# GpSimd takes over two small operations of each layer norm in a gated cross-attention kernel

## The reference

```python
x = x + tanh(g_xattn[0]) * L0_xattn(ctx, ctx, layernorm(x), ...)   # layer norm A; softmax over heads
x = x + tanh(g_ffn[0])   * L0_ffn(layernorm(x), ...)               # layer norm B; silu gate, hidden 768
x = x + tanh(g_xattn[1]) * L1_xattn(layernorm(x), ctx, ...)        # layer norm C; softmax over keys
x = x + tanh(g_ffn[1])   * L1_ffn(layernorm(x), ...)               # layer norm D; one linear map
```

```python
def _layernorm(x, axis=-1, eps=1e-05):
    m = jnp.mean(x, axis=axis, keepdims=True)
    v = jnp.var(x, axis=axis, keepdims=True)
    return (x - m) / jnp.sqrt(v + eps)
```

## Time and profile before

| | |
|---|---|
| runs before | 2554.6, 2552.17, 2556.8 us; median 2554.6 us |
| profiled execution | 2554.42 us, its span 2552.6 us |
| TensorE busy | 2463.6 us, 97% |
| VectorE busy | 2311.4 us, 91% |
| ScalarE busy | 1616.7 us, 63% |
| GpSimd busy | 1476.5 us, 58% |
| neg_mean, four norms | 64 each; A 457 ns, D 217 ns, B and C 169 ns on the mean |
| var_eps, four norms | 64 each; 156 to 161 ns |
| granted TensorE clock over the span | 0.996 |

### The profile page before, as it was taken

One profiled execution on the slowest core, in us unless ns is written; L12 is line 12 of the kernel. 1 busy time (PEld: TensorE's weight loads), 2 busy tenths in 40 slices (PEclk: granted clock), 3 DMA queues, 4 the chain that ended last, 5 costly groups with the idle time before them and its releaser, 6 DMA issues.

```text
span 2552.6 us, 70067 instructions
## 1 busy us (share of the span) xinstructions
PE 2463.6 (97%) x27972; PEld 2151.3 (84%) x27972; DVE 2311.4 (91%) x4254; ACT 1616.7 (63%) x3210; POOL 1476.5 (58%) x1806
## 2 busy tenths in 40 slices
PE   6999999999999999999999999999999999999997
PEld 5888888888888888888888888888888888888886
DVE  7889999999999999999999999999999999999974
ACT  4466666666666666666666666666666666666653
POOL 3555565565565565665665665665665665655642
PEclk9999999999999999999999999999999999999999
DMA  3000010010000010010110110110110100110100
GB/s 101 20 28 25 25 33 22 28 33 21 29 31 23 29 31 23 29 31 19 33 31 19 33 31 19 33 31 19 33 31 19 33 31 19 33 31 19 30 18 14
DMA packets 74322, 73.20 MB, mean 29 GB/s; under 512 B 6555, under 2 KB 73393, under 8 KB 74290
## 3 DMA queue, kind: packets, MB, share of 16 engines
q1 hardware_dynamic: 74290, 72.75, 9.2%
HBM read 54.90 MB, written 16.78 MB: 28 GB/s over the span
## 4 chain that ended last, share of the span: by engine, by line
PE 48%; DVE 46%; issue 3%; ACT 1%; POOL 0%; DMA 0%; SPq 0%; POOLq 0%; DVEq 0%; ACTq 0%
PE work L1849 11%; PE work L1850 9%; PE work L1851 9%; DVE m L1284 6%; DVE e L1302 6%; DVE m L1293 5%; PE scores L1952 5%; PE work L1985 5%; DVE x L1321 4%; DVE y_q L1312 3%; PE scores L1942 3%; DVE scores L1290 3%; PE work L1888 3%; PE work L1866 2%; DVE work L1298 2%
## 5 line engine op out<-in xcount | busy, mean ns | idle before, releaser
L731 ACT ACTIVATE e<-scores 120x1024 f32<-120x1024 f32 x512 | 497.4, 1023 | 133.2 <-PE scores L1952 97.0
L1849 PE MATMUL work<-xt_hi_B,w_hi 128*128 128x256 f32 x1536 | 452.4, 295 | 1.9 <-DVE xt_lo_B L1264 0.9
L1851 PE MATMUL work<-xt_hi_B,w_lo 128*128 128x256 f32 x1536 | 432.9, 282 | 0.0
L1850 PE MATMUL work<-xt_lo_B,w_hi 128*128 128x256 f32 x1536 | 432.8, 282 | 0.0
L388 POOL TENSOR_TENSOR h_lo<-h_f,h_hi 128x256 fp32r<-128x256 f32 x384 | 291.4, 772 | 219.7 <-ACT h_hi L681 219.7
L394 POOL TENSOR_TENSOR zt<-e 120x512 f32<-120x512 f32 x256 | 325.8, 1284 | 80.1 <-ACT e L731 80.1
L1849 PEld LDWEIGHTS work<-xt_hi_B,w_hi 128*128 128x128 f32 x1536 | 289.2, 188 | 58.4 <-issue 21.3
L1284 DVE TENSOR_REDUCE m<-scores 120x128 fp32r<-120x2048 f32 x128 | 291.7, 2279 | 3.1 <-PE scores L1942 3.1
L1302 DVE TENSOR_TENSOR e<-e,work 120x2048 f32<-120x2048 f32 x128 | 292.1, 2282 | 2.2
L681 ACT ACTIVATE h_hi<-h_f 128x256 fp32r<-128x256 f32 x384 | 157.1, 432 | 215.2 <-DVE h_f L1278 210.6
L1850 PEld LDWEIGHTS work<-xt_lo_B,w_hi 128*128 128x128 f32 x1536 | 289.5, 188 | 2.8
(11 more groups left out here) (213 smaller groups left out, 7299.1 us busy)
## 6 DMA issues: line engine op xcount, KB each, us to landing
x_res<-xp SPq DMA_DIRECT2D x64, 256.0 KB, 2.8
x_ln<-xp SPq DMA_DIRECT2D x64, 256.0 KB, 2.9
y<-y_out SPq DMA_DIRECT2D x64, 256.0 KB, 2.2
ctx_f_A<-cp SPq DMA_DIRECT2D x64, 128.0 KB, 2.1
ctx_f_C<-cp SPq DMA_DIRECT2D x64, 128.0 KB, 2.0
qm<-mT SPq DMA_DIRECT2D x256, 4.0 KB
e<-wi SPq DMA_DIRECT2D x3, 768.0 KB, 6.9
w_ctx<-wc SPq DMA_DIRECT2D x1, 656.0 KB
```

Source lines behind the costliest of these rows:

```text
L731: return act.activation(e[0:SC, c, 2 * h:2 * h + 2, :, :].rearrange("p a b n -> p (a b n)"), scores[0:SC, 2 * h:2 * h + 2, :].rearrange("p ...
L1849: pe.matmul(out, a_hi, b_hi_, start=first, stop=False, skip_group_check=parts)
L1850: pe.matmul(out, a_hi, b_lo_, start=False, stop=False, skip_group_check=parts)
L1851: last = pe.matmul(out, a_lo, b_hi_, start=False, stop=end, skip_group_check=parts)
```

## The change

In `moments` VectorE no longer writes neg_mean and var_eps and no longer waits for bn_aggr; what follows the norm on other engines now follows the second bn_aggr. In `root` GpSimd first adds a constant tile of epsilon to the two variances, subtracts the two means from a constant tile of zeros, waits for the addition, and then takes the power and the product as before. Two memsets fill the new tiles. The order of the work on each engine stays as it is.

```diff
--- before.py
+++ after.py
@@ -33,7 +33,7 @@
 KC = D // P
 NT = S // P
 HC = HID // P
-INIT_POOL = 9
+INIT_POOL = 11
 FIRST = 2
 STAGES_BEHIND = 0
 CONSTS = 7
@@ -106,6 +106,8 @@
         x3_biased = sb("x3_biased", [P, NT, D])
         val_bias = sb("val_bias", [P, D])
         minus_half = sb("minus_half", [P, NT])
+        eps_tile = sb("eps_tile", [P, NT])
+        zero_tile = sb("zero_tile", [P, NT])
 
         x_ln = sb("x_ln", [P, NT, D])
         x_res = sb("x_res", [P, NT, D])
@@ -365,6 +367,8 @@
         @block.gpsimd
         def _(pool):
             pool.memset(minus_half[:, :], -0.5).then_inc(s["init_pool"], 1)
+            pool.memset(eps_tile[:, :], EPS).then_inc(s["init_pool"], 1)
+            pool.memset(zero_tile[:, :], 0.0).then_inc(s["init_pool"], 1)
             pool.memset(v0_pad[:, :, :], 0.0).then_inc(s["init_pool"], 1)
             pool.memset(v1_one[:, :], 1.0).then_inc(s["init_pool"], 1)
             pool.memset(ones_k[:, :].bitcast(F32), 1.0).then_inc(s["bias_zero"], 1)
@@ -379,9 +383,12 @@
             pool.wait_ge(s["init_pool"], INIT_POOL)
 
             def root(st, t):
+                pool.tensor_tensor(var_eps[st][:, :], mv[st][:, :, 1], eps_tile[:, :], ALU.add).then_inc(s[f"ln_root_{st}"], 1)
+                pool.tensor_tensor(neg_mean[st][:, :], zero_tile[:, :], mv[st][:, :, 0], ALU.subtract)
+                pool.wait_ge(s[f"ln_root_{st}"], within(0, 2, t))
                 pool.tensor_tensor(rstd[st][:, :], var_eps[st][:, :], minus_half[:, :], ALU.pow)\
                     .then_inc(s[f"ln_root_{st}"], 1)
-                pool.wait_ge(s[f"ln_root_{st}"], within(0, 1, t))
+                pool.wait_ge(s[f"ln_root_{st}"], within(1, 2, t))
                 return pool.tensor_tensor(shift[st][:, :], neg_mean[st][:, :], rstd[st][:, :], ALU.mult)
 
             def hidden_lo(m):
@@ -1251,14 +1258,11 @@
                 for i in range(NT):
                     last = dve.bn_stats(stats[st][:, i, :], x[:, i, :])
                 last.then_inc(s[f"ln_mom_{st}"], 1)
-                dve.wait_ge(s[f"ln_mom_{st}"], within(0, 2, t))
+                dve.wait_ge(s[f"ln_mom_{st}"], within(0, 1, t))
                 dve.tensor_copy(ln_count[:, :], stats[st][:, 0, 0:1])
                 for i in range(NT):
                     last = dve.bn_aggr(mv[st][:, i, :], stats[st][:, i, :])
-                last.then_inc(s[f"ln_mom_{st}"], 1)
-                dve.wait_ge(s[f"ln_mom_{st}"], within(1, 2, t))
-                dve.tensor_scalar(neg_mean[st][:, :], mv[st][:, :, 0], -1.0, None, ALU.mult)
-                return dve.tensor_scalar(var_eps[st][:, :], mv[st][:, :, 1], EPS, None, ALU.add)
+                return last
 
             def low(out, src, hi):
                 return dve.tensor_tensor(out, src, hi.bitcast(F32), ALU.subtract)
```

## The result

The changed kernel takes 2511.6 us (median of 4 runs, 2510.54 to 2513.09) against 2554.62 us before (4 runs, 2552.17 to 2556.8): a ratio of 0.9832, 95% interval 0.9815 to 0.9849. It is 43.0 us faster. The forecast was faster, 2526 us and a range of 2518 to 2545: the sign is right, the gain is half as large again as the forecast one and lies outside the range.

A forecast was written before the change was run, and what follows sets the result against it. It took each 38.48 us pass as bound by VectorE, then TensorE, in turn, with the B chain deciding together with f1. Saving 0.49 us over 59 passes, 28.9 us off 2554.4, gave 2526 us, range 2518 to 2545.

The forecast's parts named there:

- The ceiling: TensorE's wait for xt_lo_D before product f1: VectorE savings could gain at most about 0.52 us a pass.
- 0.57 (D and C): VectorE before moments B: savings behind bn_aggr of D (0.31) and C (0.26) start x_res 0.57 us earlier.
- I take 0.35: GpSimd's root: 0.35 us from the add's start to the power's start, add slot 0.15 plus a complete subtract 0.20.
- the TensorE stretch keeps its length: TensorE's part of a pass, after transposes B and gate_up: unchanged in length, so 0.49 us is saved a pass.
- p: Time in GpSimd's root from add to power; the gain a pass is 0.57 + 0.27 - p.
- rival 1: The forecast itself: 0.38 to 0.56 us gained a pass, 2521 to 2532 us, chance 0.6.
- I count nothing: The 20 of 256 layer norms outside the loop: together under some 5 us, put at nothing.
- Rival 2: Added GpSimd work is dearer and part of the gain goes back through shift_B: 2532 to 2549 us, chance 0.16.
- rival 3: Slower: add and subtract each cost what the power costs, B chain 0.54 us later a pass, 2586 us, chance 0.04.
- Rival 4: Saved VectorE time meets another wait (x_res for wo0, or attended products), pass about 38.48 us: 2550 to 2559, chance 0.06.
- Rival 5: More than forecast: shorter first f1 product, p at 0.27, a few us outside the loop; 2514 to 2521 us, chance 0.14.
- signs named for cases 2 and 3: Add or subtract above 0.3 us, or ScalarE's shift_B wait grows and TensorE waits for xn_B or xt_lo_B.

The follow-up runs named there:

- e1: Changed kernel with only norms C and D moved to GpSimd, A and B as before the change: a pass of 37.797 us, 2509.51 us in one run.
- e2: Changed kernel with only norm A moved to GpSimd, the others as before the change: a pass of 38.442 us, 2549.70 us in one run.
- e3: Changed kernel with only norm B moved to GpSimd, the others as before the change: a pass of 38.463 us, 2549.16 us in one run.
- e8: Changed kernel with A, C and D moved and B wholly as before the change: a pass of 37.814 us, 2511.01 us, ratio 0.9831.
- e5: Changed kernel with two more GpSimd subtractions in each of roots A, C and D: a pass of 37.833 us, 2513.56 us in one run.
- e4: Changed kernel with two more GpSimd subtractions in root B alone: a pass of 38.133 us, 2529.08 us in one run.
- e7: Changed kernel, but for B VectorE writes var_eps and GpSimd negates the mean behind the power: a pass of 37.899 us, 2515.12 us, ratio 0.9847.
- e10: The changed kernel itself, run again with nothing altered: a pass of 37.834 us, 2512.34 us, ratio 0.9838.
- e6: Changed kernel with norm B's power made a multiplication, so B's scale is not the reference's: a pass of 37.420 us, 2485.90 us in one run.
- e9: Changed kernel, but for B VectorE writes var_eps and GpSimd negates the mean before waiting for it: a pass of 37.743 us, 2507.65 us, ratio 0.9818.

## Why the prediction was right in its sign and too small

Where the gain comes from was right. VectorE's stretch before xt_lo_D is what counts (e1: C and D give the whole gain), A goes into waits of VectorE (e2: the pass 0.04 us shorter), B trades a VectorE saving for a GpSimd price (e3, e8: nothing), and roots A, C and D are covered (e5). Root B decides the pass (e4).

The step that failed is the sum: three of its terms for a pass were mis-sized (0.57 us gained on VectorE, 0.08 lost in root B, nothing in the TensorE stretch: 0.49 us together, where 0.64 was measured), and the norms outside the loop, which it put at nothing, brought about 5 us. The ceiling that stood over it was wrong too. By its terms:

- *"0.57 (D and C)" before moments B.* Measured 0.60 at x_res and 0.63 at mv_B, 0.06 us a pass more. Most of this is that the step behind bn_aggr is itself a little shorter than it was: from h_f to head_max 0.31 us instead of 0.33, from x_res to mv_B 1.55 instead of 1.58.
- *"I take 0.35" for add to power.* With it root B would cost 0.08 us more than before. Measured 0.30: add and subtract each take a slot of 0.15 and the power starts as the second slot ends; the wait for the add's semaphore is over by then. That is 0.05 us a pass, within the bounds given, 0.27 to 0.43.
- *"the TensorE stretch keeps its length".* From transposes B to the next yz_q 17.21 us became 17.17: 0.04 us a pass. This is not the work of any one norm's move. By the means between 1000 and 1400 us the stretch is 17.20 us before and 17.14 to 17.15 in e1 to e5 and in e7 to e10, so also with A alone (e2) and with B alone (e3). The edits that e1, e2 and e3 share are the two new tiles and their memsets; the kernel before with these alone was not run, and the cause stays open.
- *"The ceiling of any gain on VectorE here is about 0.52 us a pass."* Wrong. f1 moved by 0.91. The 0.52 was TensorE's idle time by the modelled end of values0, and this end is not a floor: after the change f1 starts at 1222.36, while values0 is drawn until 1222.52, 0.16 later. Nor was TensorE as early as it can be: values0 starts 0.23 earlier in the pass (1243.59 - 1225.55 = 18.04 before, 1221.39 - 1203.58 = 17.81 after). The three parts, 0.52 and 0.16 and 0.23, make up the 0.91. Even then f1 starts 0.05 us behind the end of xt_lo_D (1222.31), as before, so how early TensorE could start it is still not seen. The 0.23 does not come from C and D, for e2 and e3 have 0.22 and 0.20 of it without their move; its cause is as open as that of the 0.04 above. e6 puts the pass at 37.42, 1.06 us under before. The ceiling did not move the forecast, which the B chain set. It was not kept to in the range either: the prediction's own gain, 0.57 + 0.27 - p with p from 0.27 to 0.43, runs from 0.41 to 0.57, and rival 1 is given with 0.38 to 0.56 beside a ceiling of 0.52.

In the loop that is 0.637 instead of 0.49 us a pass: 58 x 0.637 = 36.9 where the forecast had 28.9 for 59 passes.

The rest is a term put at nothing: *"Of 256 layer norms 20 are outside ... I count nothing."* The stretch before the first yz_q of the loop became 4.4 us shorter and the one behind the last 2.6. e10, the same kernel again, gives 2.0 (147.48 - 145.46) and 2.6, so some 2 us of the first number are scatter in the start: the first bn_stats of A starts at 26.7 us before and in e10 and at 25.2 after, and the granted TensorE clock over the first 140 us is 0.95 before and in e10, and 0.98 after. So 4.6 us (2.0 and 2.6) belong to the change by e10. The medians are in line with it: 43.0 us less 36.9 leaves 6.1, and e10's 41.8 less 58 x 0.647 = 37.5 leaves 4.3. The prediction's own bound was "under some 5 us"; it should have been in the sum. Which norms of the prologue and the epilogue bring it was not traced, and e2 does not show it: it is 2.5 us faster than the kernel before that was run beside it (2552.18), and 58 passes at 0.04 make 2.3 of that.

Rival 2, dearer GpSimd work, is out, and rival 3 with it: var_eps_B takes 0.196 us on GpSimd, as the product shift does. The Trainium skill, "GPSIMD Engine Reference", section "Performance versus the Vector engine", would have it at about twice VectorE's time, by an addition of 2048 elements; at 128x2 this case's rows say 1.2 times (0.196 against the 0.16 of VectorE's var_eps_B). Rival 4, another wait that takes the saving, did not happen: x_res started without a wait at 0.60 earlier. Rival 5, more than the forecast, is what happened, with a chance of 0.14, and even it ended at 2514. Of its reasons, p is 0.30, near its 0.27, and the few us outside the loop are there, but the first product of f1 did not get shorter: it takes 0.39 us after the change too, with no wait in front of it. One of the signs named for cases 2 and 3 appeared although neither happened: TensorE now waits for xn_B, because f1 came 0.91 earlier. The other half of that sign did not, for ScalarE's wait for shift_B fell from 2.3 to 1.9 us a time.

## What to carry to other kernels

Do not take a ceiling from the gap that the profile draws in front of an engine that waits: a modelled end of a matmul can lie behind the start of the next one (0.16 us here), and while an engine waits nothing shows how much earlier it could have been there (0.53 us of idle time before, 0.75 in e2, with f1 in the same place). When small operations move off a paced engine, price them per place: here two norms of four held the whole gain, one was hidden and one was a trade, which moving one or two norms at a time (e1, e2, e3, e8) told apart. Put a new small operation where its engine waits for another one (e9: a pass of 37.743 us), not between a result and the wait in front of its use (e7: 37.899).

## What the runs showed of the hardware

- On GpSimd, an instruction that waits for the one just before it starts 0.08 us after that one's end. In e7 the subtraction starts at 1224.85 and the product that waits for it at 1225.13, 0.28 us later; in the changed kernel the subtraction without a semaphore takes a slot of 0.15 us (1221.96 to 1222.11).
- VectorE starts the instruction behind two bn_aggr of 128x6 0.15 us after the start of the first (1213.83 to 1213.98), also where that instruction reads 128x512 (1219.79 to 1219.94).
- TensorE's products in the VectorE-paced stretch came a little faster, in the changed kernel and in e1 to e10 alike (278 or 279 ns in all of them). The group of the down product on the page of the changed kernel, beside 282 ns in the kernel before:

```profile
L1854 PE MATMUL work<-w_lo,h_hi 128*128 128x256 f32 x768 | 213.6, 278 | 0.0
```

Its instructions, their order and their operands are the same. The granted clock does not account for it: over the span it is 0.998 against 0.996, but from 190 to 2300 us it is 1.00 in both kernels, and the difference lies in the first 140 us. The cause stays open.
